# An attention and expert kernel on one core: four changes of order, in the prologue, at the first weight sums and in the last batch

## What is computed

```python
# step 1: cross attention, 16 heads, then eight "experts" whose mean is taken, then Wo
n = layernorm(x)
Q, K, V = n @ Wq.T + bq, ctx @ Wk.T + bk, ctx @ Wv.T + bv
out = softmax(Q K^T / sqrt(32)) V
x = x + tanh(g_xattn) * ((mean_e(out @ We[e].T + be[e])) @ Wo.T + bo)
# step 2: top-1 routing of all 4096 rows to 8 experts, 100 places each, first come first served
hs = layernorm(x)
probs = softmax(hs @ w_gate); best = argmax(probs); gate = probs[best]
place = running count of rows routed to best     # kept if place < 100
x = x + tanh(g_ffn) * gate * (hs @ w_expert + b_expert)   # only for the kept rows
```

## Time and profile before

| | |
|---|---|
| three runs | 415.05, 415.07, 415.48 us; median 415.07 |
| the profiled execution | 413.09 us, of which the span is 411.4 |
| busy in the span | PE 97%, DVE 82%, ACT 55%, POOL 41% |
| chain that ended last | PE 84%, DVE 6%, ACT 3%, issue 3% |
| granted clock of TensorE | 1.00 of full speed |

### The profile page before, as it was taken

One profiled execution on the slowest core, in us unless ns is written; L12 is line 12 of the kernel. 1 busy time (PEld: TensorE's weight loads), 2 busy tenths in 40 slices (PEclk: granted clock), 3 DMA queues, 4 the chain that ended last, 5 costly groups with the idle time before them and its releaser, 6 DMA issues.

```text
span 411.4 us, 8771 instructions
## 1 busy us (share of the span) xinstructions
PE 400.2 (97%) x3126; PEld 190.5 (46%) x3126; DVE 336.1 (82%) x683; ACT 228.3 (55%) x320; POOL 166.8 (41%) x154
## 2 busy tenths in 40 slices
PE   8999989999999999999999999999999999999987
PEld 4556554444444444444444444444444445354434
DVE  7449267886897989988998999899896688779994
ACT  5434422668465854947585485748457474774200
POOL 2028999115090347309033530803361072550460
DMA  8999981366048507824870692386059026232584
GB/s 278 325 387 398 385 320 37 81 124 169 2 102 175 199 1 160 220 95 88 148 237 3 144 228 104 71 170 235 1 131 239 4 55 174 73 114 47 107 169 148
DMA packets 65517, 63.19 MB, mean 154 GB/s; under 512 B 41765, under 2 KB 45233, under 8 KB 65475
## 3 DMA queue, kind: packets, MB, share of 16 engines
q1 hardware_dynamic: 60363, 56.19, 49.8%
q0 software_dynamic: 1632, 3.49, 3.1%
q10 hardware_dynamic: 3480, 2.96, 2.2%
HBM read 29.59 MB, written 12.98 MB: 103 GB/s over the span
## 4 chain that ended last, share of the span: by engine, by line
PE 84%; DVE 6%; ACT 3%; issue 3%; ACTq 1%; DMA 1%; SPq 0%; DVEq 0%
PE ps L840 71%; PE ps L456 7%; PE ps L588 3%; PE ps L405 2%; ACTq L1244 1%; DMA raw<-in_L_xattn_Wk_dram 1%; DVE xb L1565 1%; DVE rows L1820 1%; ACT xn L1233 1%; DVE bn_raw L1571 1%; ACT xb L1233 1%; DVE xn_lo L1808 1%; ACT woT_hi L397 0%; ACT mixT_hi L397 0%; DVE q_stack L1838 0%
## 5 line engine op out<-in xcount | busy, mean ns | idle before, releaser
L1233 ACT ACTIVATE probs<-ps 120x1024 f32<-120x1024 f32 x64 | 62.0, 1023 | 21.0 <-PE ps L840 20.9
L1599 DVE TENSOR_REDUCE neg_max<-ps 128x16 bf16<-128x1920 f32 x32 | 68.6, 2143 | 3.7 <-PE ps L840 3.7
L1985 POOL TENSOR_TENSOR attn_lo<-attn,attn_hi 128x512 f16<-128x512 f32 x28 | 31.8, 1158 | 92.0 <-ACT attn_hi L1233 92.0
L840 PE MATMUL ps<-xnT_hi,wqT_hi 128*128 128x512 f16 x128 | 48.6, 380 | 0.0
L840 PE MATMUL ps<-mixT_hi,attn_hi 128*128 128x512 f16 x128 | 48.6, 380 | 0.0
L840 PE MATMUL ps<-mixT_lo,attn_hi 128*128 128x512 f16 x128 | 48.5, 379 | 0.0
L840 PE MATMUL ps<-xnT_lo,wqT_hi 128*128 128x512 f16 x128 | 48.5, 379 | 0.0
L1993 POOL TENSOR_TENSOR xb<-xb,mix_bias 128x512 f32<-128x512 f32 x32 | 39.6, 1272 | 17.5 <-DVE cb_col L1542 17.5
L1233 ACT ACTIVATE q_hi<-ps,bias_cols 128x512 f16<-128x512 f32 x32 | 22.0, 688 | 31.5 <-PE ps L840 31.5
L840 PE MATMUL ps<-q_stack,k_stack 97*120 97x512 f16 x128 | 34.9, 390 | 0.1
L840 PE MATMUL ps<-probs,den_sel 120*32 120x256 f32 x512 | 34.1, 384 | 0.8 <-issue 0.8
(11 more groups left out here) (277 smaller groups left out, 805.6 us busy)
## 6 DMA issues: line engine op xcount, KB each, us to landing
xb<-in_x_dram SPq DMA_DIRECT2D x8, 1024.0 KB, 6.6
q_stack<-q_hi SPq DMA_DIRECT2D x48, 128.0 KB, 2.4
out_dram<-xb SPq DMA_DIRECT2D x6, 1024.0 KB, 6.5
raw<-in_L_xattn_We_dram SPq DMA_DIRECT2D x5, 1024.0 KB, 11.2
q_stack<-q_lo SPq DMA_DIRECT2D x32, 128.0 KB, 2.4
xb<-in_L_xattn_We_dram SPq DMA_DIRECT2D x3, 1024.0 KB, 9.8
k_stack<-k_scratch SPq DMA_DIRECT2D x8, 360.0 KB, 4.3
k_scratch<-k_hi ACTq DMA_DIRECT2D x16, 120.0 KB, 6.7
```

Of the source, the lines that this page charges most:

```text
L840: return e.matmul(out_, a, b, start=start, stop=stop, **kw)
L1233: return e.activation(out_, in_, func, **kw)
L1599: e.tensor_reduce(neg_max[:, :, :, g], quad[:, :, 0:NT * SK].rearrange("p j (t s) -> p t j s", t=NT), AX.X, ALU.max, negate=True).then_inc ...
L1985: e.tensor_tensor(attn_lo[:, g, :], attn[:, g, :], attn_hi[:, g, :], ALU.subtract).then_inc(s_alo, 1)
```

## The change

Four things change; no instruction is added or removed.

1. On ACT, `first_rows` moves from behind the four `woT` evacuations and the second `store_k` to ahead of the `woT` evacuations; the `wogT` evacuation moves ahead of the 12 key stores.
2. PE's `weight_sums(0, 0)` waits only for the last `mix` unit's evacuations. The wait for all six late units moves to `route_x(1)`.
3. In the last batch, PE's `value_sums(7, 0)` comes ahead of `table_token`; it takes over the wait for `read_places(6)` (`s_plr`), whose bank it overwrites.
4. `row_product(7)` comes ahead of `places(7)`.

```diff
@@ weight_sums
                 if g == 0:
                     if b == 0:
-                        prologue_over(e)
+                        for s_, n in made[("mix", NK - 1)]:
+                            e.wait_ge(s_, n)
@@ value_sums
                     e.wait_ge(s_ex, 4 * B)
+                elif (b, g) == (B - 1, 0):
+                    e.wait_ge(s_plr, B - 1)
@@ route_x
                 elif b == 1:
+                    prologue_over(e)
                     e.wait_ge(s_qhi, 4)
@@ run([B - 1]) on PE
-                (scores, 0, 1), (weight_sums, 0, 0), (table_token, -1, 0), (value_sums, 0, 0), (scores, 0, 2),
+                (scores, 0, 1), (weight_sums, 0, 0), (value_sums, 0, 0), (table_token, -1, 0), (scores, 0, 2),
...
-                (places, 0, 0), (row_product, 0, 7),
+                (row_product, 0, 7), (places, 0, 0),
@@ ACT, for i in range(N_FIRST)
+                if units[i]["done"] == made[("woT", 0)]:
+                    first_rows()
+                prepare(0, i)
                 if units[i]["done"] == made["wogT"]:
                     store_k(1)
-                    first_rows()
-                prepare(0, i)
```

## The result

| | before | after |
|---|---|---|
| median of five executions each, one chip | 415.05 us | 408.09 us |
| lowest to highest | 412.36 to 415.48 | 407.74 to 408.48 |
| the profiled execution | 413.09 us | 408.48 us |
| its span | 411.4 us | 406.7 us |

The ratio is 0.9847, with an interval of 0.9815 to 0.9878. The gain is 7.0 us between the medians. Between the two profiled executions it is 4.6 (4.7 between the spans), where 4.5 was forecast. So the question of this study is where the other 2.4 are. Of these, 2.0 are the distance of the profiled execution of before from its median, and 0.4 that of the one after from its own (408.48 against 408.09), which is within the spread of its executions.

What follows compares the result with a forecast made beforehand. PE, busy for 251.65 of 252.00 us in the middle, was taken as the bound, so gains lie in its idle times outside it. 2.0 + 0.65 + 0 + 1.85 = 4.5 us; 415.07 - 4.5 = 410.6 us, range 409.5 to 412.2.

Steps and rivals of the forecast that it cites:

- Part A: Prologue: ACT's earlier norm and wogT evacuation end PE's idle ahead of wog and v 4; 2.0 us, between -0.3 and 2.1.
- the stores: Prologue: key stores, issued later, land before PE waits for them; a rival had them land late and slow the kernel, 3%.
- `cb` didn't wait: Prologue: cb finds wog evacuated with 0.9 us of slack; a rival had cb wait or the experts' sum late, 10%.
- Part B: First weight sums: PE's 0.81 us idle goes, 0.2 returns at the gate mix; 0.65 us, between 0.4 and 0.81.
- Part C: Last batch: earlier value sums fill the wait ahead of table_token, but ACT's exponential holds the scores; 0, between 0 and 1.0.
- The rival that C pays: Last batch: batch 7's exponential isn't what holds the scores; gain 5.5 us, time 409.6 us, chance 8%.
- Part D: Near the end: row product 7 fills PE's 1.70 us idle ahead of places(7); 1.85 us, between 0.3 and 1.9.
- The sum: Whole kernel: 2.0 + 0.65 + 0 + 1.85 = 4.5 us, the same from the profiled execution or the median.

Runs made afterwards that it cites:

- part A alone: ACT's norm and wogT evacuation ahead of the key stores, in the kernel before: 411.02 us, ratio 0.9906.
- ACT's order turned round: Changed kernel with batch 7's exponential ahead of l_exp on ACT and table_values behind the value sums on PE: 409.69 us, ratio 0.9904.
- D alone: Kernel before with only row product 7 ahead of the last places: 413.16 us, ratio 0.9943.
- the kernel before once more: The kernel before, run again without an edit as a control: ratio 1.0004; its profiled execution took 414.32 us.
- the stall put back: Changed kernel, but wog also waits for the evacuations of x 1, which it doesn't need: 412.31 us, ratio 0.9930.
- without part A: Changed kernel with ACT's list of the kernel before, also called all but part A: 411.94 us, ratio 0.9929.
- the first two groups of experiments: The first four and next four experiments, run beside new executions of the kernel before with medians of 414.70 and 414.77 us.
- the last group: The last four experiments, run beside new executions of the kernel before with a median of 414.93 us.

## Why the prediction was wrong, step by step

- **Part A, 2.0:** right against executions at full clock. `v 4` is 2.11 earlier, and part A alone gains 2.1 by them. The stall's idle times of 1.63 and 0.42 both went, the stores cost nothing, and `cb` didn't wait. Against the median it gains 3.7, and the 1.6 between the two is what was missed.
- **Part B, 0.65:** right in its mechanism. 0.81 of waiting went, and 0.2 came back at the gate mix as forecast. B alone was not run; the evidence is the lead at the gate mix, 2.78, less the 2.28 that the profile of part A alone has there (99.36 for 101.64), so 0.5, or 0.7 with the 2.11 of `v 4`.
- **Part C, 0:** right, for the reason given: the exponential behind `l_exp` holds the scores. Three profiles have `table_values` within 0.08 us, with `table_token` early or late, and with ACT's order turned round the scores no longer wait. The rival that C pays would have given 409.6, closest of all to the result, by a mechanism that did not occur.
- **Part D, 1.85:** right. The trace gives 1.9, and D alone gave 1.9 at full clock, from two executions.
- **The new wait for the small DMA** was not forecast. It is hidden by the same chain as part C's gain.
- **The sum** forecast a span of 406.9 and a time of 408.6; the profiled execution after has 406.7 and 408.48.

**The step that failed** is in the sum: "It lies 2.0 below the median of the runs, 415.07, and the gain is the same from either." It is not the same. The profiled execution of before lay 2.0 below its median because the clock did not fall behind its stall. Most of its other executions have that fall, and part A takes away the idle time ahead of it, so the fall goes too.

The price of the fall is 1.7 in the trace of the kernel before once more. Between the mean of the executions at 0.995 or 0.996 and the mean at full clock it is 1.9 with the stall put back (412.65 less 410.73), 2.1 with part D alone, 2.0 without part A, and in the kernel before 1.8 (414.91 less 413.10) and 1.8 (415.32 less 413.54) beside the first two groups of experiments and 2.4 (415.22 less 412.81) beside the last. The run of before once more, with two at full clock, gives only 0.9. Beside the last group the gain of 408.25 is 4.6 from the mean at full clock, which is the forecast 4.5, and 7.0 from the mean at 0.995 or 0.996, which is the measured gain. And the idle time of PE in this place brings the fall about: filled with products, the fall is gone and the stall is not; put into the changed kernel, both are there.

The Trainium skill (TensorE: Matmul & The Clock Gate, section Part 1: The HAM clock gate) states the two levels, says that the gate goes by how busy TensorE has lately been, and that one kernel shows different numbers of slow products from run to run. This case agrees: 0.50 and 1.00 behind the same stall in two profiles. The prediction weighed no such rival, although the 2.0 us between the profiled execution and three runs within 0.43 us of each other stood in front of it.

What stays open: why the clock falls in one execution and not in another, and what in this stall matters beside its length. Behind 1.33, 1.84, 2.11 and 2.16 us at this place the clock fell in the profiled executions, behind 1.63 and 1.22 it did not. And PE idles as long near the end, 1.70 to 1.71 ahead of `places(7)`, in all six profiles that still have part D's wait, and there the clock stayed at 1.00 in each. Open too: four executions of the kernel before, at 0.991 or 0.992, took 416.86 to 417.67, some 2 us more again, and none of them was profiled.

## What to carry to other kernels

When the profiled execution lies further from the median than the runs lie from each other, the profile lacks something that most runs have, and a sum made against it can't simply be moved to the median; look for a stall that a fall of the granted clock could follow, and forecast both cases. A gap of one or two us in a stream of products can cost as much again in slower products behind it, as the one at 51 did and the one at 393 did not, so a change that closes such a gap may have two terms. A wait that a fixed chain ends (here `l_exp` and the exponential) is worth nothing to remove, and hides equally well what is lost ahead of it.

## What the runs showed of the hardware

- Behind one idle time of PE of 1.3 to 2.2 us in the prologue, the granted clock was 0.50 for some 3 to 4 us in four profiles (before once more, part D alone, all but part A, the stall put back) and 1.00 in that of before; 38 of 51 executions of the kernel before and 7 of 12 with the stall put back had a mean clock of 0.991 to 0.996, short of full clock by at least about one such stretch; where, only the profiled ones show. Products of 512 columns then started 0.43 us apart in place of 0.215. It cost 1.7 in the trace of before once more, and 1.8 to 2.4 between most means.
- Behind 1.70 to 1.71 us of idle time near the end the clock stayed at 1.00 in six profiles of six.
- Nine products that nobody reads, 2.11 us of them, in that prologue stall kept the mean clock at 1.00 in all six executions.
- ACT's DMA issues run ahead of its arithmetic: the first key store was issued at 43.08, while the evacuation that it follows in the queue, `sum_hi`, started at 44.63.
- A DMA of 16 KB landed in 2.6 to 4.0 us, in the same place of the same kernel.
